# Moving the next block's input layernorm ahead of the receptance matmuls, with four sets of layernorm scratch

## The reference

```python
x = x + _layernorm(attn(_layernorm(x), Wq, bq, Wk, bk, Wv, bv, Wo, bo))
x = x + _layernorm(ffn(_layernorm(x), W_r, W_k, W_v, mu_r, mu_k))
# attn: 16 heads of 64, rope on q and k, causal band of 512 keys before the query
# ffn, with x_prev = x shifted by one token:
xr = mu_r * x + (1.0 - mu_r) * x_prev
xk = mu_k * x + (1.0 - mu_k) * x_prev
r = jax.nn.sigmoid(xr @ W_r)
k_act = jnp.square(jax.nn.relu(xk @ W_k))
out = r * (k_act @ W_v)
```

## Time and profile before

| | us |
|---|---|
| median of the runs | 5711.75 (5711.65 to 5711.86) |
| the profiled execution | 5720.1 |
| its span on the slowest core, core 1 | 5718.4 |
| spans of the 8 cores | 5694.3 to 5718.4 |
| PE busy | 3205.2 (56%) |
| DVE busy | 2527.1 (44%) |
| ACT busy | 2121.1 (37%) |
| POOL busy | 1064.6 (19%) |

### The profile page before, as it was taken

One profiled execution on the slowest core, in us unless ns is written; L12 is line 12 of the kernel. 1 busy time (PEld: TensorE's weight loads), 2 busy tenths in 40 slices (PEclk: granted clock), 3 DMA queues, 4 the chain that ended last, 5 costly groups with the idle time before them and its releaser, 6 DMA issues.

```text
span 5718.4 us, 54149 instructions; the slowest of 8 cores (5694.3 to 5718.4 us)
## 1 busy us (share of the span) xinstructions
PE 3205.2 (56%) x11840; PEld 1240.2 (22%) x11840; DVE 2527.1 (44%) x3689; ACT 2121.1 (37%) x3905; POOL 1064.6 (19%) x900
## 2 busy tenths in 40 slices
PE   0345737468373764737556374673836367374673
PEld 0112313123121221312222131221312122131231
DVE  2354525445263443534436354443534544354443
ACT  0142533425333352533524243362433326343262
POOL 0011212212111121211211122131221212122021
PEclk9958567575676757667576675856768585675857
DMA  6513022140321302123031321302113130321301
GB/s 192 154 44 101 3 80 68 45 103 1 83 65 52 96 30 77 41 63 85 31 90 31 89 56 45 103 8 88 52 45 103 45 103 1 88 59 45 103 5 62
DMA packets 251425, 376.92 MB, mean 66 GB/s; under 512 B 149730, under 2 KB 149730, under 8 KB 251108
## 3 DMA queue, kind: packets, MB, share of 16 engines
q1 hardware_dynamic: 185060, 163.72, 11.5%
q0 software_dynamic: 33792, 134.22, 7.8%
q10 hardware_dynamic: 32256, 75.51, 3.4%
HBM read 264.33 MB, written 75.50 MB: 59 GB/s over the span
## 4 chain that ended last, share of the span: by engine, by line
PE 34%; ACT 20%; DVE 20%; issue 8%; DMA 8%; POOL 5%; SPq 3%; ACTq 2%; DVEq 1%; POOLq 0%
PE pb L477 8%; ACT pk L449 7%; PE pb L626 5%; PE pb L442 5%; PE pb L391 4%; DVE ybuf L489 4%; ACT vext L249 4%; ACT vext L252 4%; PE pb L654 4%; PE pb L533 3%; DVE ax L589 3%; SPq L173 3%; DMA sinb<-sind 2%; POOL pk L460 2%; POOL ybuf L703 2%
## 5 line engine op out<-in xcount | busy, mean ns | idle before, releaser
L489 DVE RECIPROCAL ybuf<-pb 1x512 bf16<-1x512 f32 x256 | 858.1, 3352 | 755.7 <-PE pb L477 747.1
L449 ACT ACTIVATE pk<-pb,neg 128x512 bf16<-128x512 f32 (+3 forms) x1792 | 945.8, 528 | 282.7 <-PE pb L442 30.8
L626 PE MATMUL pb<-WS,qx 128*128 128x512 bf16 x1024 | 274.4, 429 | 1159.5 <-DVE qx L596 1098.5
L442 PE MATMUL pb<-qx,krot 64*128 64x512 bf16 (+3 forms) x1792 | 673.6, 431 | 311.2 <-ACT pk L449 255.4
L477 PE MATMUL pb<-pk,vext 128*65 128x128 bf16 (+3 forms) x2368 | 520.1, 402 | 79.1 <-DVE ax L502 38.9
L464 POOL TENSOR_TENSOR pk<-pk,tri4s 128x512 bf16<-128x512 bf16 x256 | 294.2, 1149 | 756.9 <-ACT pk L449 756.9
L460 POOL TENSOR_TENSOR pk<-pk,tri0s 128x512 bf16<-128x512 bf16 x192 | 220.7, 1149 | 1124.3 <-ACT pk L449 1124.3
L654 PE MATMUL pb<-ax,WS 128*128 128x512 bf16 x1024 | 261.2, 420 | 291.1 <-ACT urt L661 291.1
L340 PE MATMUL pb<-hfm,Wwq 128*128 128x512 bf16 x1024 | 241.6, 391 | 295.7 <-DMA hfm<-hstage 225.1
L626 PEld LDWEIGHTS pb<-WS,qx 128*128 128x128 bf16 x1024 | 105.9, 108 | 1324.8 <-issue 1244.0
L254 DVE TENSOR_SCALAR nmt<-ssum 128x1 f32<-128x1 f32 x256 | 39.4, 154 | 792.8 <-ACT vext L249 792.4
(11 more groups left out here) (97 smaller groups left out, 3898.6 us busy)
## 6 DMA issues: line engine op xcount, KB each, us to landing
xsl<-x SPq DMA_DIRECT2D x128, 512.0 KB, 4.6
WS<-wo_bf POOLq DMA_DIRECT2D x16, 2048.0 KB, 11.9
WS<-wr_bf POOLq DMA_DIRECT2D x16, 2048.0 KB, 20.5
WS<-wk_bf POOLq DMA_DIRECT2D x16, 2048.0 KB, 10.6
WS<-wv_bf POOLq DMA_DIRECT2D x16, 2048.0 KB, 11.0
out<-ybuf ACTq DMA_DIRECT2D x64, 512.0 KB, 2.7
hstage<-htm ACTq DMA_DIRECT2D x64, 256.0 KB, 2.6
cosb<-cosd SPq DMA_DIRECT2D x64, 256.0 KB, 6.5
```

What stands on the lines that cost most here:

```text
L442: qlo=qlo, qhi=qhi: e.matmul(pb[bk][:, qlo:qhi], ksrc[po:po + 64, BS * md + 128 * tc:BS * md + 128 * (tc + 1)], qx[po:po + 64, BS * md + q ...
L449: texp = cop("scalar", lambda e, bk=bk, c=c, qlo=qlo, qhi=qhi, pku=pku: e.activation(out=pku[:, BS * c + qlo:BS * c + qhi], in_=pb[bk][:, ...
L489: t_rc = cop("vector", lambda e, rb=recipb[uslot], ub=ub: e.reciprocal(rb, pb[ub][64:65, :]), waits=[t_av, buf.get(("recip", uslot)), prev ...
L626: ins = e.matmul(pb[bk][:, :], qx[:, BS * ci + 128 * tj:BS * ci + 128 * (tj + 1)], WS[1][:, D * ci + BS * hh:D * ci + BS * (hh + 1)], star ...
```

## The change

The call of `planA(it + 1)` moves from behind the r stage to ahead of it, right behind L612. And the one-column buffers exist four times, chosen by the slice's number; a token `("lnset", i)` makes the first pass of a slice wait for the normalisation that last used its set.

```diff
-    ssum = sb("ssum", [128, 1], F32)
-    nmt = sb("nmt", [128, 1], F32)
...
+    lnt = [dict(ssum=sb("ssum%d" % i, [128, 1], F32), nmt=sb("nmt%d" % i, [128, 1], F32),
+                svt=sb("svt%d" % i, [128, 1], F32), vart=sb("vart%d" % i, [128, 1], F32),
+                sdt=sb("sdt%d" % i, [128, 1], F32), rst=sb("rst%d" % i, [128, 1], F32))
+           for i in range(4)]
...
-    def ln_stats(xap, waits):
+    def ln_stats(xap, waits, si):
         sink = lnsink[0]
+        T = lnt[si]
+        ssum, nmt, svt = T["ssum"], T["nmt"], T["svt"]
+        vart, sdt, rst = T["vart"], T["sdt"], T["rst"]
         t1 = cop("scalar", lambda e, sink=sink: e.activation(
             out=sink, in_=xap, func=AF.Identity, accum_out=ssum[:, :]),
-            waits=list(waits), tok=True)
+            waits=list(waits) + [buf.get(("lnset", si))], tok=True)
...
-            t_rs = ln_stats(xsl[sl][:, :], [t_x1[j]])
+            t_rs, nmt, rst = ln_stats(xsl[sl][:, :], [t_x1[j]], j)
...
+            buf[("lnset", j)] = t_ln[j]
...
         buf["hfm"] = h2l_tok
+        if it + 1 < niter:
+            pendingA = planA(it + 1)
 
 
         wr_users = []
...
                 t_rsg.append(trs)
                 bank_free[bk] = trs
-
-        if it + 1 < niter:
-            pendingA = planA(it + 1)
 
         t_wv2 = stream_weight("wv2", 1, wr_users)
```

More of the change, by code:

```diff
@@ L262, in ln_stats @@
         t6 = cop("vector", lambda e: e.reciprocal(rst[:, :], sdt[:, :]), waits=[t5], tok=True)
-        return t6
+        return t6, nmt, rst
     def stream_weight(wn, slot, after):
@@ L294, in planA @@
                           xin[rows0a + 128 * j: rows0a + 128 * (j + 1), :], waits=w)
-            t_rs = ln_stats(xsl[sl][:, :], [t_x1[j]])
-            t_ln[j] = cop("vector", lambda e, sl=sl, j=j: e.tensor_scalar(
+            t_rs, nmt, rst = ln_stats(xsl[sl][:, :], [t_x1[j]], j)
+            t_ln[j] = cop("vector", lambda e, sl=sl, j=j, nmt=nmt, rst=rst: e.tensor_scalar(
                 htm[:, D * j:D * (j + 1)], xsl[sl][:, :], nmt[:, :], rst[:, :], ALU.add, ALU.mult),
                 waits=[t_rs, buf.get("htm")], tok=True)
+            buf[("lnset", j)] = t_ln[j]
         t_hw = [dma("scalar", "hw", hstage[128 * j:128 * (j + 1), :], htm[:, D * j:D * (j + 1)],
@@ L547, in build_core @@
             sl = tj % 2
-            t_rs = ln_stats(aof[sl][:, :], t_oev)
-            tt1 = cop("vector", lambda e, sl=sl: e.tensor_scalar(
+            t_rs, nmt, rst = ln_stats(aof[sl][:, :], t_oev, tj)
+            tt1 = cop("vector", lambda e, sl=sl, nmt=nmt, rst=rst: e.tensor_scalar(
                 scr[:, :], aof[sl][:, :], nmt[:, :], rst[:, :], ALU.add, ALU.mult),
@@ L552, in build_core @@
             buf[("aof", sl)] = tt1
+            buf[("lnset", tj)] = tt1
             t_y[tj] = cop("gpsimd", lambda e, sl=sl, tj=tj: e.tensor_add(
@@ L563, in build_core @@
         for j in range(4):
-            t_rs = ln_stats(ybuf[:, D * j:D * (j + 1)], [t_y[j]])
-            t_h2.append(cop("vector", lambda e, j=j: e.tensor_scalar(
+            t_rs, nmt, rst = ln_stats(ybuf[:, D * j:D * (j + 1)], [t_y[j]], j)
+            th2j = cop("vector", lambda e, j=j, nmt=nmt, rst=rst: e.tensor_scalar(
                 htm[:, D * j:D * (j + 1)], ybuf[:, D * j:D * (j + 1)], nmt[:, :], rst[:, :],
-                ALU.add, ALU.mult), waits=[t_rs, t_hw[-1]], tok=True))
+                ALU.add, ALU.mult), waits=[t_rs, t_hw[-1]], tok=True)
+            t_h2.append(th2j)
+            buf[("lnset", j)] = th2j
         t_h2w = [dma("scalar", "hw", h2stage[128 * j:128 * (j + 1), :], htm[:, D * j:D * (j + 1)],
@@ L697, in build_core @@
             sl = tj % 2
-            t_rs = ln_stats(aof[sl][:, :], t_fev)
-            tt1 = cop("vector", lambda e, sl=sl: e.tensor_scalar(
+            t_rs, nmt, rst = ln_stats(aof[sl][:, :], t_fev, tj)
+            tt1 = cop("vector", lambda e, sl=sl, nmt=nmt, rst=rst: e.tensor_scalar(
                 scr[:, :], aof[sl][:, :], nmt[:, :], rst[:, :], ALU.add, ALU.mult),
```

## The result

The changed kernel takes 5603.1 us (median, 5568.4 to 5666.9); the kernel before, run beside it, 5711.75 (5704.6 to 5745.4). The ratio is 0.9785, with a 95% interval of 0.9751 to 0.9820: 2.15% faster, or 5589 us from the median before, where I had said 5586 in a range of 5562 to 5628. That there is no gain lies outside the interval; a gain a little under 2% lies inside. In some executions of most kernels here, before or changed, one die was granted 0.65 to 0.68 of the clock in place of 0.70 and took up to 110 us longer, and the ratios leave out the longest of these but not all.

What follows compares the result with a forecast made beforehand. No engine is always busy; k matmuls wait 19.4 us a block for ACT's layernorm. Saving 9.66 less 1.30 us, 15 times, takes 125.4 from 5720.1; less 8.35 to the median, 5586 us, range 5562 to 5628.

Steps and rivals of the forecast that it cites:

- the pass over slice 2 at 7.30: Input layernorm on ACT: its pass over slice 2 starts 7.30 us after the first r matmul, with a 3.7 us load.
- r slice 1 at 18.55: r stage on PE: matmuls of slice 1 start 18.55 us after the first r matmul, behind layernorm and first sigmoid.
- The k stage at 33.27: PE: the k matmuls start 33.27 us after the first r matmul, a slow restart in the r stage included.
- the first v matmul at 48.50: PE: k stage runs through without stalls, so the first v matmul starts 48.50 us after the first r matmul.
- The charge for the slow restart, 2.37: r stage from slice 1: 2.37 us added because PE's matmuls run slower after standing some 13 us.
- 9.66 us saved up to the v stage: From first r to first v matmul: 48.50 us in place of 58.16, saving 9.66 us in each block.
- 1.30 us given back by the table load: v stage on ACT: its first square root now needs a table load, costing 1.30 us uncovered in each block.
- The sum, 8.36 a block: Whole block: 9.66 us saved less 1.30 given back is 8.36 us, 15 times, 125.4 us over the run.
- that the four sets let ACT run ahead: Rival: ACT runs ahead of DVE, the r stage goes as before, saving 307 us for 5405; chance 0.02.
- That the clock falls once more: Rival: second slow stretch between r slice 1 and k stage, 1.96 us a block, 5615 us; chance 0.25 with load bounds.
- The late weights: Rival: `W_v` lands late for the v stage, 6.0 us a block, 5676 us, chance 0.06; slower beyond 22.9 us, chance 0.03.
- another of my signs of being wrong: Start of the v stage: the prediction is wrong if `L679` waits for a DMA.

Runs made afterwards that it cites:

- the third experiment: Changed kernel plus one unused square root on ACT behind the ReLUs, ahead of the v stage, to fetch the table early; 0.9686 of the kernel before, median 5551.8 us.
- the statistics hoisted: Changed kernel with all layernorm passes ahead of the small operations, x slices 2 and 3 in `aof` buffers, `hstage` stores by SP; 0.9488 of the kernel before, 5445.0 us.
- all three together: Changed kernel with layernorm passes written first, four PSUM bank pairs for the r stage and an unused early square root; 0.9265 and, rerun, 0.9314 of the kernel before.

## Why the prediction was right

The direction, the size and the mechanism held. Step by step:

- *The square root of slice 0 at 1.62 us, the pass over slice 2 at 7.30, r slice 1 at 18.55.* In block 9 these were 1.80, 6.97 and 18.38; the mean of the last is 18.23. The load of slice 2 took 3.34 us on the mean, where I had taken 3.7; in 7 of 120 blocks it took over 4.
- *The k stage at 33.27, the first v matmul at 48.50.* 32.75 and 48.29. The charge for the slow restart, 2.37, fits the 6.02 - 3.61 = 2.41 of block 9. I had worked it out from two blocks: the 12.72 us are of block 13, the granted clock of 0.84 of block 9, whose matmuls took 12.70.
- *9.66 us saved up to the v stage.* 58.20 - 48.29 = 9.91. That my 58.16 is so near the mean of all blocks was luck: the two blocks it rests on lie 1.4 above and 1.5 below.
- *1.30 us given back by the table load.* 1.35, and the third experiment won it back. The rule of the Trainium skill that I had weighed against it did not hold here. Taken by the letter, one of my signs of being wrong came, that the v stage grows by more than 1.3: I had set it at the cost that I forecast, with no room for the 0.05.
- *The sum, 8.36 a block.* 9.91 - 1.35 = 8.56. The whole block fell by 345.13 - 335.49 = 9.64. The 1.08 beyond lie in stages that the change doesn't touch: 0.46 between the first rope operation and the v projection, 0.61 in the rest. The kernel with four sets and no move shows 0.38 and 0.26 of the same kind against before, so such differences come without the change; I can't say more of their cause. They make up most of what the profiled pair shows beyond the forecast, 5720.1 - 5568.4 = 151.7 against 125.4 us. The ratio gives 123, and the last column 135 with an error of 2.7.

The rivals: that the four sets let ACT run ahead is excluded, by the move alone and by the 22.21 us that ACT still waits. That the clock falls once more did not come: from r slice 1 to the k stage it is 32.75 - 18.23 = 14.52 us on the mean and at most 15.3, and the sum had 14.72 with one slow restart alone. The late weights did not decide in the changed kernel (landing at 45.08 on the mean for a use at 48.29), but in 3 of 120 blocks they were late, which by the letter is another of my signs of being wrong, and one step further, with the statistics hoisted, in 45. The forecast's margin of 3.5 us was 3.2, and it was right to call it thin.

One thing I had not seen although it stood in the same rows: that 13 of the 19.4 us of stall only changed place, because the r stage had a single pair of banks. The sum had the wait in it, but I treated it as given. The banks are a small edit and, behind the move, worth more than the move itself.

## What to carry to other kernels

When a chain of small steps moves from one stage to another, ask which buffer the waiting engine is short of in the new place: by the ratios the move gave 2.2%, the move with more PSUM banks 5.7%, while the banks alone gave 1.6%. Separate scratch buffers buy nothing while the instructions stand in an order that serialises them; the gain came when the passes of all slices were written ahead of the first dependent step, together with two more buffers for `x`. And a function table that changes hands can be fetched with one unused operation in idle time, for 1.3 us here each time.

The best kernel of the study, all three together, ran at 0.9265 and 0.9314 of the kernel before, and at about 0.95 of the changed one.

## What the runs showed of the hardware

- In its first profile, the kernel with all three edits was granted 0.81 of the clock over the whole k stage of block 9 (core 3), on a stretch in which PE was busy throughout, and its 64 matmuls took 16.97 us in place of 13.98 at the same place in the second profile. The mean granted clock of the cores was 0.672 to 0.690 against 0.705 to 0.709. The clock's record has a level of 0.812 for 601 to 1177 us on each core of the first profile, and for none on any core of the second, of the same program. The Trainium skill, "TensorE: Matmul & The Clock Gate", section "Seeing it yourself", names such a share, 13 of 16, as a current limit of a die on which three or more cores run dense matmuls. The 0.81 agrees; whether the current is the cause no run here shows.
- A 2 MB weight load that took 10.3 us on the mean in the kernel before took 13.7 in the one with hoisted statistics, where it runs from 22.6 to 36.3 us beside the last of the transposing DMAs (to 27.4) and all the `cosb` and `sinb` loads (23.4 to 37.1). The transposes alone don't do it: with all three edits it runs from 16.8 to 28.1 among transposes (12.8 to 30.4), mostly ahead of those loads (from 26.8), and takes 11.4. No run moves the `cosb` and `sinb` loads alone.
- A table load starts 0.08 us behind the end of a ReLU and is followed by its square root 0.01 us behind its own end (16 of 16 times in the kernel with the early square root).
